# The combine stage's landing tiles filled by ScalarE, and the graph stage's first gathers issued ahead of its constants

## The reference, cut to what matters

```python
h = (x_flat @ W_gat).reshape(M, HEADS, NUM_EXPERTS)
...
e = jax.nn.leaky_relu(a_src[src] + a_dst[dst], negative_slope=0.2)
e_max = jax.ops.segment_max(e, dst, num_segments=M)
ee = jnp.exp(e - e_max[dst])
denom = jax.ops.segment_sum(ee, dst, num_segments=M)
alpha = ee / (denom[dst] + 1e-16)
msg = h[src] * alpha[:, :, None]
agg = jax.ops.segment_sum(msg, dst, num_segments=M).reshape(M, HEADS * NUM_EXPERTS) + b_gat
scores = _layernorm(agg, ln_gamma, ln_beta).reshape(M, HEADS, NUM_EXPERTS).mean(1)
topk_s, topk_i = jax.lax.top_k(scores, TOP_K)
w = jax.nn.softmax(topk_s, axis=-1)
...
    out = out + g[..., None] * (hh @ W2[ei] + b2[ei])
```

## Time and profile before

| | us |
|---|---|
| median of 3 runs (lowest, highest) | 10792.27 (10772.9, 10792.55) |
| the profiled execution's own time | 10787.32 |
| its span, from first to last instruction | 10785.5 |
| graph stage, from 4812.2 | 5248.5 |
| combine stage, from 10060.8 to the end | 724.7 |

### The profile page before, as it was taken

The page is one execution under the profiler, slowest core; times in us unless marked ns, Lnnn a source line. Parts: engine busy times, 40 slices in busy tenths (PEclk is TensorE's granted clock), DMA queues, the critical chain, the costliest instruction groups (busy, mean ns, idle before and its releaser), DMA issues. The chain is left out here.

```text
span 10785.5 us, 111540 instructions
## 1 busy us (share of the span) xinstructions
PE 4563.0 (42%) x31813; PEld 2715.7 (25%) x31813; DVE 5474.9 (51%) x14162; ACT 3929.5 (36%) x9657; POOL 6184.6 (57%) x6259
## 2 busy tenths in 40 slices
PE   0011777777758997873222222223223223223000
PEld 0011555555544444541111111111111101101000
DVE  9987999999986775541121121121121112112487
ACT  0011888888854554332121111112112112112255
POOL 0000555555532224667777777777777777777675
PEclk9755999999978998876666666666666666666555
DMA  0000111111121223543222222222222222222366
GB/s 20 2 0 34 40 39 38 39 41 38 39 78 55 62 62 100 141 121 55 44 46 49 44 46 49 44 42 53 44 42 53 44 42 53 44 42 48 134 250 244
DMA packets 1326096, 663.81 MB, mean 62 GB/s; under 512 B 1058255, under 2 KB 1239100, under 8 KB 1320764
## 3 DMA queue, kind: packets, MB, share of 16 engines
q1 hardware_dynamic: 1142396, 576.49, 19.5%
q0 software_dynamic: 183104, 80.22, 5.7%
HBM read 344.86 MB, written 313.71 MB: 61 GB/s over the span
## 5 line engine op out<-in xcount | busy, mean ns | idle before, releaser
L1832 POOL DMA_INDIRECT gr_rec<-rec,gr_idx x4096 | 3954.2, 965 | 1248.8 <-issue 1248.0
L1853 PE MATMUL gr_p_h<-gr_tT,gr_w 128*128 128x512 f32 x1568 | 849.4, 696 | 3671.7 <-ACT gr_hT L1887 3638.7
L1972 DVE TENSOR_SCALAR gr_pen<-gr_same 128x64 f32<-128x64 f32 x64 | 13.7, 213 | 3170.6 <-DMA gr_rec<-rec,gr_idx 3170.6
L1853 PEld LDWEIGHTS gr_p_h<-gr_tT,gr_w 128*128 128x128 f32 x1568 | 347.6, 227 | 4154.9 <-ACT gr_hT L1887 3723.8
L544 POOL TENSOR_TENSOR at_sq<-at_qk 128x256 f32<-128x256 f32 x392 | 290.2, 740 | 1844.1 <-ACT at_qk L594 1843.9
L1900 ACT ACTIVATE gr_ee<-gr_dd 128x512 f32<-128x512 f32 x64 | 40.3, 629 | 3588.0 <-DVE gr_dd L1991 3588.0
L1858 PE MATMUL gr_p_y<-gr_hT,gr_w 128*128 128x512 f32 x1568 | 688.9, 592 | 0.0
L1952 DVE STREAM_TRANSPOSE gr_z<-gr_yb 128x2048 f32<-128x2048 f32 x98 | 226.5, 2311 | 902.8 <-issue 491.5
L1887 ACT ACTIVATE gr_hT<-gr_p_h,gr_b 128x512 f32<-128x512 f32 x784 | 517.6, 688 | 191.7 <-PE gr_p_h L1853 191.0
L2140 POOL DMA_INDIRECT cb_a<-scan,cb_idx x392 | 499.0, 1273 | 133.7 <-issue 122.4
L1340 POOL DMA_INDIRECT adst<-co_rec,co_idx x448 | 424.5, 948 | 223.3 <-issue 123.1
(11 more groups left out here) (358 smaller groups left out, 13212.1 us busy)
## 6 DMA issues: line engine op xcount, KB each, us to landing
y<-gr_z SPq DMA_DIRECT2D x392, 256.0 KB, 5.4
cb_y<-y SPq DMA_DIRECT2D x28, 3584.0 KB, 13.2
gr_rec<-rec,gr_idx POOLq DMA_INDIRECT x4096, 2.3
scan<-gr_out SPq DMA_DIRECT2D x64, 768.0 KB, 3.8
at_xs<-in_x_win SPq DMA_DIRECT2D x56, 448.0 KB, 3.8
x<-at_x SPq DMA_DIRECT2D x56, 448.0 KB, 4.2
ff_x<-x SPq DMA_DIRECT2D x56, 448.0 KB, 3.4
x<-ff_x SPq DMA_DIRECT2D x784, 32.0 KB
```

The source lines that it names most:

```text
L1832: nc.gpsimd.indirect_dma_start(out=rec[s][:, j, :], out_offset=None, in_=rec_dram, in_offset=bass.IndirectOffsetOnAxis(ap=idx[s][:, j:j + ...
L1853: nc.tensor.matmul(p_h[m % 4][:, :], w1[:, P * m:P * (m + 1)], tT[b.k][:, :], start=True, stop=True).then_inc(S["hp"], 1)
```

## The change

Three edits in the combine stage: `cb_a` is filled by ScalarE instead of GpSimd; the gathers take their indices straight from `cb_end`, and `cb_idx` and its semaphore go; `cb_end` has a semaphore of its own (`end_in`), which is all that GpSimd waits for besides the fill. The tiles of blocks 0 and 1 are filled ahead of ScalarE's loop; that of block t+2 in the step of block t, behind four of its six products. Two edits in the graph stage: the first index tile is the first transfer that SyncE issues, ahead of its wait for `set`; the gather of `gr_headr` stands behind the 64 of chunk 0, and VectorE's wait for it stands in the work on chunk 0.

```diff
@@ graph_and_experts, SyncE
             def _(sp):
+                sp.dma_start(idx[0][:, :], src_dram.rearrange("(p e) -> p e", p=P)[:, 0:CH]).then_inc(S["ix0"], 16)
                 sp.wait_ge(S["set"], 1)
...
-                        sp.dma_start(idx[s][:, :], src_dram.rearrange("(p e) -> p e", p=P)[:, cols]).then_inc(S[f"ix{s}"], 16)
+                        if p.t >= 0:
+                            sp.dma_start(idx[s][:, :], src_dram.rearrange("(p e) -> p e", p=P)[:, cols]).then_inc(S[f"ix{s}"], 16)
@@ graph_and_experts, GpSimd
-
-                pool.wait_ge(S["set"], 2)
-                nc.gpsimd.indirect_dma_start(out=headr[:, :], out_offset=None, in_=rec_dram,
-                                             in_offset=bass.IndirectOffsetOnAxis(ap=headi[:, 0:1], axis=0)).then_inc(S["head_in"], 16)
+                        if p.t == 0:
+                            pool.wait_ge(S["set"], 2)
+                            nc.gpsimd.indirect_dma_start(out=headr[:, :], out_offset=None, in_=rec_dram,
+                                                         in_offset=bass.IndirectOffsetOnAxis(ap=headi[:, 0:1], axis=0)).then_inc(S["head_in"], 16)
@@ graph_and_experts, VectorE
-                v.wait_ge(S["head_in"], 16)
-
...
                         if first:
+                            v.wait_ge(S["head_in"], 16)
@@ combine, SyncE
-                for dst, src in ((end[:, :], end_dram), (cst[:, :, :], d["g_ln"]), (order[:, :, :, :], d["order"])):
+                sp.dma_start(end[:, :], end_dram).then_inc(S["end_in"], 16)
+                for dst, src in ((cst[:, :, :], d["g_ln"]), (order[:, :, :, :], d["order"])):
@@ combine, GpSimd
-                idx = [sb(f"idx{i}", [P, FB], I32) for i in range(2)]
-                copied = ctx.enter_context(nc.semaphore("cb_copied"))
-                pool.wait_ge(S["consts_in"], 48)
-                pool.wait_ge(S["set"], 1)
+                pool.wait_ge(S["end_in"], 16)
...
-                        p.wait("f", -2, NF)
-                        p.wait_lot("ga", -2, FB * 16)
-                        pool.sem_inc(S["passed"], 1)
-
-                        nc.gpsimd.tensor_copy(a[s][:, :, :], low[:, :, :])
-                        nc.gpsimd.tensor_copy(idx[s][:, :], end[:, bass.ds(p.t * FB, FB)]).then_inc(copied, 1)
-                        pool.wait_ge(copied, p.t + 1)
+                        p.wait("fill", 0)
                         pool.sem_inc(S["passed"], 1)
                         for j in range(FB):
+                            n = p.t * FB + j
                             nc.gpsimd.indirect_dma_start(out=a[s][:, j, :], out_offset=None, in_=scan_dram,
-                                                         in_offset=bass.IndirectOffsetOnAxis(ap=idx[s][:, j:j + 1], axis=0),
+                                                         in_offset=bass.IndirectOffsetOnAxis(ap=end[:, n:n + 1], axis=0),
@@ combine, ScalarE
                 act.wait_ge(S["set"], 1)
+
+                for i in range(2):
+                    nc.scalar.activation(a[i][:, :, :], low[:, :, :], ACT.Copy).then_inc(S["fill"], 1)
...
                         product(p, 1, 0)
+                        if p.has(2):
+                            nc.scalar.activation(a[p.slot(0)][:, :, :], low[:, :, :], ACT.Copy).then_inc(S["fill"], 1)
@@ combine, VectorE
-                v.wait_ge(S["consts_in"], 48)
+                v.wait_ge(S["consts_in"], 32)
```

More of the change, by code:

```diff
@@ L2076, in combine @@
         S = {n: ctx.enter_context(nc.semaphore("cb_" + n)) for n in (
-            "consts_in", "set", "in0", "in1", "xy0", "xy1", "pre", "f", "sq", "act", "sum", "prod", "out0", "out1", "passed", "passed_sp")}
+            "end_in", "fill", "consts_in", "set", "in0", "in1", "xy0", "xy1", "pre", "f", "sq", "act", "sum", "prod", "out0", "out1", "passed", "passed_sp")}
         S.update(zip(("ga0", "ga1"), d["soft"][11:13]))
```

## The result

The changed kernel takes 10966.31 us (median of 6 runs, 10955.49 to 10970.25), the kernel before 10790.72 us (6 runs beside it): the ratio is 1.0165, with a 95% interval from 1.0152 to 1.0178. It is slower by 175.6 us. The forecast was 10948, with a range from 10920 to 10990, so the result lies inside the range, 18 us above the forecast.

The account below looks back on a forecast made before the run. GpSimd's gathers were taken to set the graph stage, with GpSimd issuing ahead in combine. Twelve longer combine periods (+168.2), the combine start (-3.8) and the graph stage (-7.9) gave +156.5 on 10792.3, rounded to 10948 us, range 10920 to 10990.

Parts of the forecast that it names:

- graph stage: Graph stage: first gather 9.2 us earlier, head gather costing 1.30 us within the stream, net 7.9 us earlier.
- first gather of combine, after its entry: Combine start: first gather at 10063.3 instead of 10065.64, after ScalarE's table load, fill and hand-over, 2.3 us earlier.
- start of VectorE on block 1: Combine start: 2.3 us from the first gather plus 1.5 us from the shorter gap before block 1, together 3.8 us.
- line 2219 to the next block's first gather: Combine, blocks 2 to 13: 1.84 to the exponential, 16.84 for it and 56 products, 0.76 fill, 0.5 hand-over: 19.9 us.
- a block of gathers: Combine: 28 gathers take 36.16 us undisturbed plus 3.9 us beside the second half of VectorE's work, 40.1 us.
- landing: Combine: from a block's last gather's end to VectorE's line 2219, 1.43 us, the value for a quiet queue.
- twelve periods against 569.8: Combine, blocks 1 to 13: twelve periods of 61.5 us make 738.0 where 569.8 stood, +168.2 us.
- The hand-over: Combine: from the end of ScalarE's fill to GpSimd's first gather, taken as 0.5 us between 0.3 and 0.86.
- rival B: Combine: the late `cb_y` load still precedes the last gathers, long landings stay, up to 5.7 us a block, 11016 us; chance 0.08.
- Rival A: Combine: the fill does not hold GpSimd up and the kernel is faster, 29 us off, 10763 us; chance 0.04.
- Rival D: Combine: gathers stay as slow as before in full, 3.9 + 4.3 us a block, 52 us more, 11000; chance 0.04.
- The signs named: Combine: 20 us idle before blocks, exponential every 61 us, mean gather about 1.14 us; graph stage's last gather 8 us earlier.

Follow-up runs that it names:

- e3: The changed kernel with the fill for block t+2 moved ahead of the exponential of block t+1 in ScalarE's queue: 10783.83 us, ratio 0.9983.
- e8: The changed kernel with the fill for block t+3 placed behind the inverse deviation of block t+1, in the step of block t: 10768.09 us, ratio 0.9976.
- e4: The changed kernel with the fill directly behind the exponential of block t+1, ahead of the products: 10908.27 us, ratio 1.0099.
- e1: The kernel before with the graph stage's two edits alone, its combine stage left as before: 10794.38 us, ratio 0.9996.
- e7: The changed kernel with each large VectorE sum of line 2295 made a reduction of the same length over one input tile: 10923.9 us, timed once.
- e6: The changed kernel with the six large VectorE sums of a block (line 2295) cut to one element each: 10905.5 us, timed once.

## Why the prediction was right, point by point

The direction, the mechanism and the place were right: the fill's place in ScalarE's queue ties each block's gathers to the landing of the block before and to 56 products. e3 shows it by moving the fill alone, and e8 again with another place. The median came out 18 us over the forecast. Every size below missed to the same side (a cost larger than forecast, or a gain smaller), so no miss hid another. By the terms, in the profiled executions:

| term | forecast | measured |
|---|---|---|
| graph stage | -7.9 | -7.7 without the gathers' own spread |
| first gather of combine, after its entry | -2.3 | -1.6 |
| start of VectorE on block 1 | -3.8 | -2.1 |
| line 2219 to the next block's first gather | 19.9 | 20.14 |
| a block of gathers | 40.1 | 40.85 |
| landing | 1.43 | 1.46 |
| twelve periods against 569.8 | +168.2 | +183.4 |
| line 2219 of the last block to the end | 0 | +0.5 |

Between the two profiled executions the span grew by 178.3 us, 21.8 more than forecast: 15.2 in the twelve periods, 1.7 at the start of block 1, 0.5 at the end, 2.7 in the graph stage (2.5 of them its gathers' busy time), and 1.7 because this execution came into the stage later. The medians show 18 of them: I took a median 5 us above the profiled execution, and here it was 0.7 above.

**The hand-over.** The fill took 0.75 us as sized from the earlier trace rows. From its end to the gather there are 0.86 us; I took 0.5 between bounds of 0.3 and 0.86, and the upper bound was the value. At the start of the combine stage it was not the fill that came last, as I had it, but the transfer of `cb_end`. The chain of waits there (start, us, what) and the timeline of the same place:

```profile
...
10057.17 2.38 DMA cb_end<-end
...
10060.45 0.34 POOL cb_a L2135
...
```

```profile
...
10057.17 0.33 SPq L2085 DMA_DIRECT2D cb_end<-end  x1
...
10058.47 1.42 ACT L2146 ACTIVATE cb_a<-cb_low 128x672 f32<-128x672 f32 x2
...
10060.45 1.03 POOL L2135 DMA_INDIRECT cb_a<-scan,cb_end  x1 [14.65 <-ACT cb_a L2146]
...
```

The first of the two fills began at 10058.47 and takes 0.75 us, so it was done by 10059.22; the transfer landed at 10059.55, and 0.90 us later the gather started, 3.28 us after the entry instead of 2.55. The bracket in the timeline names the fill, but the chain names the transfer, and e8 bears it out: there the transfer took 2.62 us instead of 2.38, and the first gather came 3.53 us after the entry.

**The gathers.** This is the largest part of the miss. I took the slowdown in the second half of VectorE's work, 3.9 us, from the earlier trace rows, where gathers already run when that half begins. In the change they begin at a fixed point in it, and a block loses 4.7 us: 1.6 in a gather beside line 2297, 0.8 beside the single sum of line 2295, 1.7 beside the pair, and the rest in small amounts. What a gather loses depends on where it starts, for one that is held up ends 0.87 us behind the instructions beside it, whenever it began, while another may pass between them: a gather at 10220.72, inside the same 14 instructions of line 2297, took only 1.14 us. So the sum of a window does not carry over exactly. That is 0.75 x 12 = 9 us.

**A pause that I left out.** In three of the twelve periods (blocks 4, 8 and 12) GpSimd stands still behind its first gather:

```profile
...
10281.76 1.06 POOL L2135 DMA_INDIRECT cb_a<-scan,cb_end  x1 [21.55 <-ACT cb_a L2169]
10285.00 2.14 POOL L2135 DMA_INDIRECT cb_a<-scan,cb_end  x1 [2.18 <-issue]
...
```

Those periods last 63.8 us instead of 62.4, 4 us in all. The trace of before had these pauses as well; they are in its 569.8 us, but not in my 36.16 + 3.9.

**The start of block 1.** Its landing took 2.23 us in this execution instead of 1.43, which with the late first gather (0.7) makes 1.5 of the 1.7 us between -2.1 and -3.8. Why that landing was longer is open.

**The landing** stayed at 1.42 to 1.53 us in blocks 2 to 13: rival B did not come. The load that decides it was issued 42.4 us after line 2219 as forecast, here in block 3:

```profile
...
10241.65 0.43 SPq L2113 DMA_DIRECT2D cb_y<-y  x1
...
```

The longest landing of such a load was 15.6 us, which makes 58.0, and the last gather ends 61.0 us after line 2219. The reasoning fits e4 too, which brings the last gathers behind the load and has 8 us there. **Rival A** is e3 and e8: where the fill comes in time, the kernel is 0.17 to 0.24% faster; the 29 us that I gave it were, in the trace of e8, 23 in the combine stage (724.7 to 701.6) and 7.2 in the graph stage by the same account as in e1. **Rival D** did not come: a block of gathers takes 40.85 us, and D asked for 44.4.

**The signs named.** The mean gather fell to 1.14 us and the idle time ahead of a block is 21.6 us, as said. ScalarE's exponential starts every 62.4 to 63.8 us instead of 61. The graph stage's end is 5.2 us earlier by its own entry, not 8; the forecast shows only after the gathers' busy time is taken off.

**Two bounds.** The 5 us of the hand-over and the 15 us of spread make 10928 to 10968, not 10972; and a landing of 2.9 instead of 1.7 us makes 6.7 of the 7.9, not 6.5. Neither enters the forecast.

**The rule weighed.** The Trainium skill, SBUF — State Buffer, Who interferes with whom: that an instruction with two inputs in SBUF meets a GpSimd instruction that reads SBUF, and that a reduction never does, agrees with e7 (1.00 us beside the reduction, 1.76 beside the sum). The page infers that `tensor_tensor` leaves the making of descriptors alone. An indirect gather as a whole is held up by it all the same; whether in the reading of its indices or in the making of its descriptors, no run here shows.

## What to carry to other kernels

Moving a small job to an engine with spare time moves it into that engine's queue, and it inherits every wait ahead of it. Before placing it, ask which instruction ahead waits for the very engine that you want to free; here 0.75 us of work behind such a wait cost 176 us, and the same work at a place that is reached in time gained 28 (e8, 10796.21 to 10768.09), both with the graph stage's 7 to 8 us in them. And a producer that is released early collides with other things: compare the pause that goes with the transfers and the shared inputs that it then meets.

## What the runs showed of the hardware

- An indirect gather issued by GpSimd takes 1.00 us alone in the combine stage. Beside a large sum with two input tiles it takes up to 2.77 us, beside a row of 14 small ones up to 3.10 us (10618.91 in the kernel before); beside a reduction with one input and the length of the large sum it stays at 1.00.

```profile
...
10617.38 3.76 DVE L2297 SCALAR_TENSOR_TENSOR cb_x<-cb_y,cb_gate,cb_x 128x128 f32<-128x128 f32 x14
...
10618.91 3.10 POOL L2140 DMA_INDIRECT cb_a<-scan,cb_idx  x1 [0.30 <-issue]
...
```

- In the combine stage of every kernel here GpSimd pauses behind the 113th, the 225th and the 337th gather: for 2.18 us in the change, 0.7 in e4, 1.5 in e6, up to 3.98 in e8 (the 0.30 us between any two gathers included). The 4096 gathers of the graph stage have no such pause. The cause is open; it was not tried.
- A gather that had to wait for a semaphore starts 0.84 to 0.91 us after what released it, whether that was ScalarE's fill, GpSimd's own copy or a transfer; between two gathers that wait for nothing there are 0.30 us.
- The entry into the graph stage (VectorE's second memset) lay at 4811.0 to 4822.4 us in the profiled executions, though all these kernels are alike up to there. Within this case, effects under some 10 us have to be read from spans of stages.
